# Graph network on one core, last stage: variances of two chunks at a time, one chunk turned per slot, two relu additions moved to VectorE

## What is computed

```python
    x = x + relu(out)                      # out: the convolution's sums, scaled by dinv
    h = jnp.maximum(_layernorm(x, axis=-1), 0.0)
    # L1: agg = segment_sum(edge_attr, dst); u is one row, the same for all nodes
    model_in = jnp.concatenate([h, agg, u[batch]], axis=1)
    z = jax.nn.relu(model_in @ W1 + b1)
    z = jax.nn.relu(z @ W2 + b2)
    x = x + (z @ W3 + b3)
```

## Time and profile before

| | |
|---|---|
| median of 3 runs | 803.67 us (803.18 to 804.12) |
| the profiled execution | 811.0 us, of which the span is 809.0 us |
| busy share of the span: PE, DVE, ACT, POOL | 89%, 74%, 57%, 25% |
| last stage | from 731.6 us, 77.4 us |
| in it, busy POOL (L1536 and L1545) | 15.5 us and 15.6 us, 13 each |

### The profile page before, as it was taken

One profiled execution on the slowest core, in us unless ns is written; L12 is line 12 of the kernel. 1 busy time (PEld: TensorE's weight loads), 2 busy tenths in 40 slices (PEclk: granted clock), 3 DMA queues, 4 the chain that ended last, 5 costly groups with the idle time before them and its releaser, 6 DMA issues. The chain is left out here.

```text
span 809.0 us, 22403 instructions
## 1 busy us (share of the span) xinstructions
PE 723.4 (89%) x9074; PEld 587.8 (73%) x9074; DVE 596.2 (74%) x1211; ACT 463.5 (57%) x865; POOL 204.2 (25%) x184
## 2 busy tenths in 40 slices
PE   0878564799999999999999999999999999994897
PEld 0656554588888888888888887878787878884554
DVE  5997953977778778777877778787787788733642
ACT  1442625666666666666666665666565656635862
POOL 3402970222222222112222212212222112203622
PEclk9986655899999999999999999999999999996999
DMA  6200610555555555555555544555555455350012
GB/s 166 78 1 3 234 39 1 165 195 182 184 193 195 194 193 181 173 178 185 193 194 194 187 156 177 195 182 161 177 194 194 154 173 193 130 148 11 27 52 81
DMA packets 64866, 119.57 MB, mean 148 GB/s; under 512 B 3077, under 2 KB 22723, under 8 KB 64807
## 3 DMA queue, kind: packets, MB, share of 16 engines
q1 hardware_dynamic: 64246, 117.89, 44.6%
q0 software_dynamic: 576, 1.16, 0.6%
HBM read 115.84 MB, written 4.03 MB: 148 GB/s over the span
## 5 line engine op out<-in xcount | busy, mean ns | idle before, releaser
L1262 ACT CAST counts_sb<-ps_counts 128x588 f16<-128x588 f32 x540 | 350.2, 650 | 219.8 <-PE ps_counts L1398 186.2
L1406 PE MATMUL ps_product<-counts_sb,table_sb 128*128 128x240 f16 x2646 | 442.3, 264 | 0.0
L1398 PE MATMUL ps_counts<-key_hot,lo_hot 128*128 128x147 bf16 x2160 | 410.6, 231 | 14.2 <-DVE key_hot L1301 11.4
L1296 DVE TENSOR_TENSOR lo_hot<-src_lo,iota_key 128x1024 bf16<-128x1024 f16 x270 | 186.1, 689 | 106.2 <-PE ps_counts L1398 101.7
L1398 PEld LDWEIGHTS ps_counts<-key_hot,lo_hot 128*128 128x128 bf16 x2160 | 206.7, 98 | 73.7 <-issue 43.7
L1406 PEld LDWEIGHTS ps_product<-counts_sb,table_sb 128*128 128x128 f16 x2646 | 243.4, 97 | 10.6
L1252 POOL TENSOR_SCALAR place_hot<-iota_c,slot_now 128x96 f32<-128x96 f32 x81 | 117.5, 1451 | 470.2 <-PE ps_product L1431 448.1
L1301 DVE TENSOR_TENSOR key_hot<-key,iota_key 128x1176 bf16<-128x1176 f16 x270 | 208.8, 773 | 0.0
L1421 PE MATMUL ps_sums<-attr,attr_hot 128*32 128x128 f32 x3240 | 122.7, 279 | 0.0
L1421 PEld LDWEIGHTS ps_sums<-attr,attr_hot 128*32 128x32 f32 x3240 | 79.0, 109 | 26.0 <-issue 25.1
L1312 DVE TENSOR_TENSOR attr_hot<-rel,iota_w 128x640 f32<-128x640 int16 x81 | 67.0, 827 | 0.0
(11 more groups left out here) (271 smaller groups left out, 585.4 us busy)
## 6 DMA issues: line engine op xcount, KB each, us to landing
attr<-in_edge_attr_dram SPq DMA_DIRECT2D x80, 1280.0 KB, 5.9
acc<-in_x_dram SPq DMA_DIRECT2D x4, 768.0 KB, 8.4
attr<-in_x_dram SPq DMA_DIRECT2D x12, 256.0 KB, 5.2
out_dram<-y_ring SPq DMA_DIRECT2D x12, 256.0 KB, 2.2
src_padded<-in_src_dram SPq DMA_DIRECT2D x1, 805.7 KB, 7.7
attr<-in_edge_attr_dram SPq DMA_DIRECT2D x2, 320.0 KB, 3.0
attr<-in_edge_attr_dram SPq DMA_DIRECT2D x1, 640.0 KB
raw_d<-in_dst_dram SPq DMA_DIRECT2D x1, 540.0 KB
```

What stands on the lines that cost most here:

```text
L1262: act.copy(counts_sb[s % 2][:].rearrange("p h (n t) -> p h n t", n=WN) [:, :, :, k * QUAD:(k + 1) * QUAD], ps_counts[n % 2][:, :, 0:KEYS]. ...
L1296: v.tensor_tensor(lo_hot[:, n % 2], src_lo[:, tiles].rearrange("p (b c) -> p b c", c=2).unsqueeze(2) .to_broadcast(whole), iota_lo[:].unsq ...
L1398: ins = pe.matmul(ps_counts[quad % 2][:, c, 0:KEYS], lo_hot[:, held, pair, :, q % 2], key_hot[:, held, pair, :, q % 2], start=True, stop=True)
L1406: ins = pe.matmul(ps_product[side][:, 0:SLOTS], table_sb[:, h, low, :], counts_sb[side][:, h, :], start=(part == 0), stop=(part == 2 * NB ...
```

## The change

Chunks are turned one per slot (chunks 4 to 10 in slots 0 to 6, 11 and 12 in slot 7) rather than two. The variance is found for two chunks at a time: six groups (chunks 0 and 1, 2 and 3, and so on; the last has 10 to 12), measured at the end of slots 0, 2, 4, 6, 8 and normal from slots 1, 3, 5, 7, 9; the first ahead of slot 0. The relu additions of chunks 0 and 1 are made by DVE, each just ahead of the chunk's statistics. POOL waits, for each of its additions, for the additions before it.

```diff
--- before.py
+++ after.py
@@ -1501,11 +1501,12 @@
                 return buffers[:, c % 2, 0:width(c) * P]
 
 
-            TURNED_IN = {-1: range(0, 4), 0: range(4, 6), 1: range(6, 8), 2: range(8, 10), 3: range(10, 12),
-                         4: range(12, CHUNKS)}
-            GROUPS = [slice(0, 4 * BC), slice(4 * BC, 8 * BC), slice(8 * BC, NB)]
-            MEASURED_IN = {2: 1, 5: 2}
-            NORMAL_IN = {3: 1, 6: 2}
+            TURNED_IN = {-1: range(0, 4), 7: range(11, CHUNKS)} | {s: (s + 4,) for s in range(0, 7)}
+            FIRST_OF = [*range(0, CHUNKS - 1, 2)]
+            GROUPS = [slice(BC * c, NB if c == FIRST_OF[-1] else BC * (c + 2)) for c in FIRST_OF]
+            MEASURED_IN = {c - 2: k for k, c in enumerate(FIRST_OF) if k}
+            NORMAL_IN = {c - 1: k for k, c in enumerate(FIRST_OF) if k}
+            ADDED_BY_DVE = range(0, 2)
             M1_AT, M2_AT, M3_AT, Y_AT = 1, 2, 3, 4
             SLOTS_ALL = range(-1, CHUNKS + Y_AT)
 
@@ -1530,9 +1531,12 @@
                     pool.memset(xs[:, FB, :], 0.0).then_inc(zeroed, 1)
                     for s in SLOTS_ALL:
                         for c in TURNED_IN.get(s, ()):
+                            if c in ADDED_BY_DVE:
+                                continue
                             if c == CHUNKS - 1:
                                 pool.wait_ge(tail_in, 16)
                             pool.wait_ge(relu_ready, c + 1)
+                            pool.wait_ge(x1_ready, c)
                             pool.tensor_tensor(chunk(xs, c), chunk(xs, c), slot(relu_ring, c), ALU.add)\
                                 .then_inc(x1_ready, 1)
                         if M3_AT <= s < CHUNKS + M3_AT:
@@ -1577,11 +1581,18 @@
 
                     v.wait_ge(b1u_done, 1)
                     v.tensor_tensor(b1u[:], ps_3[0][:, 0:1], B1, ALU.add).then_inc(b1u_ok, 1)
-                    for c in TURNED_IN[-1]:
+                    for c in ADDED_BY_DVE:
+                        v.wait_ge(relu_ready, c + 1)
+                        if c >= 1:
+                            v.wait_ge(x1_ready, c)
+                        v.tensor_tensor(chunk(xs, c), chunk(xs, c), slot(relu_ring, c), ALU.add).then_inc(x1_ready, 1)
                         ins = take_stats(c)
                     link(ins)
                     find_variance(GROUPS[0])
                     find_shift(0)
+                    for c in TURNED_IN[-1]:
+                        if c not in ADDED_BY_DVE:
+                            ins = take_stats(c)
                     for s in SLOTS_ALL:
                         if s >= Y_AT:
                             c = s - Y_AT
@@ -1623,7 +1634,7 @@
                         ins.then_inc(relu_ready, 1)
 
                     def normalize(c):
-                        act.wait_ge(norm_ok, 1 + (c >= 4) + (c >= 8))
+                        act.wait_ge(norm_ok, min(c // 2 + 1, len(GROUPS)))
                         if c >= 2:
                             act.wait_ge(h2_turned, c - 1)
                         for k in range(width(c)):
```

## The result

The changed kernel takes **810.56 us** (median of 5 runs, 808.88 to 812.05) against 803.62 us before (5 runs, 803.18 to 804.12). The ratio is 1.0087, 95% interval 1.0069 to 1.0106: slower by 6.9 us. The forecast was 809.3, range 803.3 to 811.5.

The account below looks back on a forecast made before the run. The last stage was taken as bound by a chain of waits through ScalarE and PE, 4.26 us a slot. From 803.67 us, -2.85 and +9.0 gave +6.1, lowered towards +5.3 to +5.6: 809.3 us, range 803.3 to 811.5.

Parts of the forecast that it names:

- the opening: Last stage, from first relu to normalising chunk 0: 1.35 us earlier, with the variance's last half running after POOL's second addition.
- the ramp: Slots 0 to 3, each with one relu chunk less: slot 4 begins 2.85 us earlier than before, the opening included.
- a loop over relu, addition, x3 and y: Slots 4 to 9: a new loop over two slots, 12.25 us with the variance held, against 8.52 before.
- holds: A running POOL addition or x3 stalls DVE's small operations with two SBUF operands; 1.15 us each, two in a pair's variance.
- Slots 4 to 9: Six slots of the last stage: 34.8 us against 25.81 before, +9.0, in pairs of 12.2, 12.3 and 10.3.
- the sum of +6.1: Whole kernel: -2.85 up to the start of slot 4, +9.0 in slots 4 to 9.
- a variant in which three operations pass together: A variance's first three operations go through together on getting the port; each pair loses one hold less, giving +5.3.
- rival (c): PE's clock stays low through slot 1 as well: +2, 811.3 us; chance included in the forecast's 0.60.
- Rival (a): POOL's holds on DVE's small operations don't come: +1.1, 804.8 us; chance 0.17.
- Rival (b): Slots 4 to 9 stay at PE's own pace, x3 coming in time for y: -3.1, 800.5 us; chance 0.11.
- The marks: Signs in the last stage's profile: normalising near 740.0, operations over 1 us ending with POOL's additions, y waiting for x3.

Follow-up runs that it names:

- e5: The changed kernel with PE repeating the transposes of h four times more in slots 5, 7 and 9; 809.92 us, ratio 1.0075 to the kernel before.
- e3: The changed kernel without DVE's two additions, POOL making all relu additions; 812.13 us, ratio 1.0086 to the kernel before.
- e6: The changed kernel with each variance's six small operations replaced by one aggregating instruction per block; 806.47 us, ratio 1.0032 to the kernel before.
- e1: The changed kernel with POOL making x3 ahead of the relu addition in each slot; 803.35 us, ratio 0.9991 to the kernel before.
- e2: The changed kernel with y moved to the end of DVE's slot, behind the variance; 803.07 us, ratio 0.9983 to the kernel before.

## Why the prediction was right

It was right in place, sign and mechanism: the gain of the opening and the ramp, then its loss to a loop over relu, addition, x3 and y with holds in it. In size it was 1.3 us too low (+5.6 forecast, +6.9 measured, within the range). Two steps of it were not right, and one nearness is luck.

**The opening** gave 1.70 us where I had 1.35. It went as laid out: POOL's second addition ends 6.88 us after the first T, as forecast, the first half of the variance runs before that and the last half after it. The last half and the steps to the normalising were 0.35 us shorter than I had rounded them. DVE's additions took 0.69 and 0.67 us, as taken.

**The ramp** gave 3.24 us at h(4) where I had 2.85; the difference is the opening's.

**Slots 4 to 9** were to take 34.8 us. With PE's clock up they take 34.29 (e5), in pairs close to the layout's; the loop is there step by step in that kernel's chain. The variance of a pair was held twice, as in the sum of +6.1, and is 2.85 us long (754.93 to 757.78) where I had summed 3.15.

**Luck.** From +6.1 I had gone down to +5.6 for a variant in which three operations pass together and each pair loses one hold less; it gives +5.3. That e5's stage shows +5.31 does not bear the variant out. The variances in its slots 4 and 6 were each held twice. The number comes from elsewhere: h(4) 0.3 us earlier than laid out, the three pairs together 0.5 us shorter. The step from +6.1 to +5.6 had no ground in what happened.

**The term that was missing** is PE's clock behind the first slots. I had it as rival (c), in slot 1 after the opening, where it did not last (0.85 in the microsecond from 738). For later slots I had put it at nothing. But waiting 2.7 us for M2 made it fall again in slot 5 of the profiled execution, for 3.0 us. Some of this comes back: after the longer slot POOL was ahead, the next variance met no addition, and h(6) to h(8) took 9.51 us instead of 12.1. Then slots 8 and 9 took 11.85 instead of 10.2. In sum 36.39 against 34.29 us, +2.1. The medians of the change and of e5 differ by 1.0 us, which is not clear of noise, so how often the second fall comes in the other runs stays open. The profiled executions of the change, twice, and of e3 had it; that of e5, made to avoid it, did not.

**The profiled execution** was forecast at 816.6 us and took 811.97. I had added the +5.6 to the 811.0 of the profile before, whose last stage began 6.4 us later in the span.

**Rival (a)**, no holds: out, with seven operations over 0.5 us. e6 comes near its condition, with no hold on a variance and some on shifts: +2.5 us, and +1.8 in the stage, where (a) has +1.1. **Rival (b)**, slots at PE's own pace: wrong for this order, since x3 did not come in time for y (1.2 us behind the third product in slot 4), and right up to h(8) for e1 and e2, which differ by one exchange. There the stage ends 0.6 and 1.2 us early rather than the 3.1 I gave it. That price was too high by two terms: h(4) is only 3.2 us early with the holds in the opening and ramp, not the 5.0 of a layout without any, and slots 8 and 9 take 9.5 and 8.9 us.

**The marks.** Seen: normalising at 733.18, 7.98 us after the first T (predicted 8.33); held operations ending with POOL's; root as the head of z1's wait; y waiting for x3. Not seen as said: of the third and fourth groups (counted from 0, measured in slots 4 and 6) the fourth had no hold in this execution (in e3 and e5 it has two), and h(4) to h(6) took 15.0 us, not near 12, by the clock.

## What to carry to other kernels

In this kernel an earlier start was kept only once no in-order queue behind it carried a loop longer than the slot of PE, the engine that bounds the stage. When work is spread thinner over slots, write down for every queue what now stands behind the newest item; here POOL's x3 stood behind the relu just made, and y, statistics, root and M2 behind x3, and exchanging two instructions was worth 8 us. A step that nobody needs soon (y) goes to the end of a slot; a step that another queue waits for (T) goes into the bound engine's wait.

## What the runs showed that I had not expected

A POOL instruction holds more of DVE than operations with two SBUF operands: the `tensor_scalar` at L1569, one 32-bit SBUF operand of 8 elements, took 1.20 us beside POOL's addition and 1.12 us beside its x3, and 0.17 us elsewhere. The reciprocal, the aggregation of e6, statistics, copy and y (one operand in PSUM) were not held. The Trainium skill has it (page SBUF — State Buffer, SBUF: two separate sides, with page VectorE: DVE Perf Modes, The perf-mode tier table): instructions in a two-port mode take the shared port as well, and `tensor_scalar` on 32-bit SBUF data is among those that have one. I had used only the half on two SBUF inputs; the trace agrees with both.

Where two POOL instructions follow each other directly, one operation of DVE passed between them: in slots 4 and 5 of the change the second of the variance was held by the addition, the third took 0.16 us and the fourth was held by x3. In the opening two passed, behind a held first one, and there POOL has a gap: two additions take 2.67 us, not 2.49 to 2.50. The gap comes from the change itself, by which each addition waits for the one before it, and not from DVE: e6 has the same 2.67 us with only the aggregation at that place, which is not held. What DVE costs POOL is small here: the addition that starts together with the mean (754.93) took 1.30 us, 1.31 in e5, against 1.27 in e6. POOL costs DVE up to all of its own 1.27.

PE's clock, which in the kernel before fell only at the start of the stage and at its very end, fell once or twice more in three profiled executions (0.50 in slots 5 or 7, and 9), each time where PE had waited over 2.3 us for M2. Not each such wait did it: 2.34 us in slot 9 of the first execution and 2.86 in slot 5 of e3 left it at 1.00. With 1.76 us of repeated transposes in the wait it stayed at 1.00 throughout (e5).
